# Keys of both head groups in one buffer, three key transfers a group, and the batch loop written out, in a two-layer attention kernel

## The reference

```python
# layer 0
xn = (x - mean) / jnp.sqrt(var + EPS) * gamma
qkv = jnp.einsum('oc,bcn->bon', w_qkv, xf)
sim = jnp.einsum('bhdi,bhdj->bhij', q, k) * scale
sim = sim + bias[None]
attn = _stable_softmax(sim)
out = jnp.einsum('bhij,bhdj->bhdi', attn, v)
out = jnp.einsum('oc,bcn->bon', w_out, out).reshape(B, C, H, W)
x1 = out + residual
# layer 1
attn = softmax(jnp.einsum('bno,bom->bnm', f, g), axis=2)
y = gamma1 * jnp.einsum('bci,bij->bcj', hh, attn) + x1
```

## Time and profile before

| | us |
|---|---|
| median of three runs | 1881.58 |
| lowest, highest | 1879.25, 1883.2 |
| span of the profiled execution | 1881.0 |

### The profile page before, as it was taken

The page is one execution under the profiler, slowest core; times in us unless marked ns, Lnnn a source line. Parts: engine busy times, 40 slices in busy tenths (PEclk is TensorE's granted clock), DMA queues, the critical chain, the costliest instruction groups (busy, mean ns, idle before and its releaser), DMA issues. The chain is left out here.

```text
span 1881.0 us, 23267 instructions
## 1 busy us (share of the span) xinstructions
PE 1642.2 (87%) x6545; PEld 805.5 (43%) x6545; DVE 1498.6 (80%) x2218; ACT 1388.9 (74%) x2043; POOL 0.2 (0%) x4
## 2 busy tenths in 40 slices
PE   6645989989988998989988999889989999889988
PEld 2133343535444453535444353535435354435424
DVE  4235988888878988789878989789878988789853
ACT  1135887878778887788778787778778787779853
POOL 0000000000000000000000000000000000000000
PEclk8667968999999999999999999999999999989999
DMA  1395103301042104301043102501043101500000
GB/s 57 58 221 156 33 25 105 110 19 39 24 138 77 57 1 127 111 1 57 24 108 107 57 1 85 149 5 57 1 128 110 43 15 53 142 20 26 16 30 23
DMA packets 72905, 123.04 MB, mean 65 GB/s; under 512 B 24042, under 2 KB 38954, under 8 KB 72746
## 3 DMA queue, kind: packets, MB, share of 16 engines
q1 hardware_dynamic: 72756, 121.29, 22.7%
HBM read 78.66 MB, written 44.13 MB: 65 GB/s over the span
## 5 line engine op out<-in xcount | busy, mean ns | idle before, releaser
L1117 DVE CUSTOM_DVE_ANT_0 biased<-psum,bias_lines_sb 128x1024 f32<-128x1024 f32 x512 | 618.0, 1222 | 209.1 <-issue 129.1
L915 ACT ACTIVATE biased<-biased,nmax 128x1024 f32<-128x1024 f32 x512 | 587.2, 1147 | 188.9 <-DVE nmax L1117 183.7
L1131 DVE TENSOR_TENSOR biased<-psum,bias_lines_sb 128x1024 f32<-128x1024 f32 x512 | 599.1, 1221 | 47.7 <-PE psum L715 37.1
L932 ACT ACTIVATE probs<-biased 128x1024 f32<-128x1024 f32 x512 | 536.0, 1056 | 132.7 <-DVE biased L1131 118.8
L688 PE MATMUL psum<-k_tail,q_stack 96*128 96x256 f32 x512 | 272.8, 533 | 120.3 <-DVE nmax L1117 50.6
L715 PE MATMUL psum<-q_stack,k_main 98*128 98x512 f32 x768 | 302.9, 502 | 38.9 <-DVE nmax L1117 15.1
L742 PE MATMUL psum<-probs,vT 128*32 128x512 f32 x2048 | 292.6, 642 | 4.9 <-DVE st L1008 2.7
L715 PEld LDWEIGHTS psum<-q_stack,k_main 98*128 98x128 f32 x768 | 137.2, 205 | 257.9 <-issue 112.6
L688 PEld LDWEIGHTS psum<-k_tail,q_stack 96*128 96x128 f32 x512 | 102.8, 201 | 305.7 <-DVE nmax L1117 172.5
L690 PE MATMUL psum<-k_main,q_stack 96*128 96x512 f32 x512 | 216.3, 422 | 0.0
L633 PE MATMUL psum<-probs 128*128 128x512 f32 x384 | 186.6, 592 | 0.0
(11 more groups left out here) (91 smaller groups left out, 1409.2 us busy)
## 6 DMA issues: line engine op xcount, KB each, us to landing
q_stack<-q_parts SPq DMA_DIRECT2D x96, 256.0 KB, 5.6
k_parts<-st SPq DMA_DIRECT2D x16, 1024.0 KB, 4.7
q_parts<-st SPq DMA_DIRECT2D x16, 1024.0 KB, 4.0
k_main<-k_parts SPq DMA_DIRECT2D x48, 256.0 KB, 5.3
xn<-in_x_dram SPq DMA_DIRECT2D x8, 1024.0 KB, 8.6
x<-in_x_dram SPq DMA_DIRECT2D x8, 1024.0 KB, 11.2
out_dram<-x SPq DMA_DIRECT2D x8, 1024.0 KB, 4.0
bias_lines_sb<-bias_lines SPq DMA_DIRECT2D x32, 240.0 KB, 20.6
```

Of the source, the lines that this page charges most:

```text
L915: nc.scalar.activation(biased[:, m % BIASED, :], biased[:, m % BIASED, :], ACT.Exp, scale=-1.0, bias=nmax[:, m:m + 1], accum_out=rowsum[:, ...
L932: nc.scalar.activation(probs[:, n % P_SLOTS], biased[:, n % BIASED, :] .rearrange("p (i n) -> p i n", i=2), ACT.Exp).then_inc(SEMS["probs_ ...
L1117: nc.vector.tensor_tensor_reduce(biased[:, m % BIASED, :], pair(bank_of(g, first, ("rows", m))), bias_lines[:, g * HG + h, a0:a0 + N], -1. ...
L1131: nc.vector.tensor_tensor(biased[:, n % BIASED, :].rearrange("p (i n) -> p i n", i=2), psum[:, bank:bank + 2, :], bias_lines[:, g * HG + 2 ...
```

## The change

`k_main` and `k_tail` become one buffer `k_stack`, with all 1024 keys of both groups. `k_in` is three transfers of 512 KB, issued in one go after `k_out`; its only wait on readers is for a columns phase of the batch before. A row tile has two products of 512 columns instead of three of 256, 256 and 512. In SP's program `k_out` and `k_in` of group 1 now stand ahead of the load of `xn`, and those of the next batch's group 0 stand whole in the rows phase of group 1. The loop over batches 1 to 6 is written out, with constant waits. The wait for `lines_loaded` is left out after the first batch.

```diff
-        KMAIN = 3 * N // 4
-        k_main = sb("k_main", [KS + 2, HG, KMAIN], F32R)
-        k_tail = sb("k_tail", [KS + 2, G, HG, N - KMAIN], F32R)
+        k_stack = sb("k_stack", [KS + 2, G, HG, N], F32R)
...
-        K_DMAS = 3 * 3 * 16
+        K_DMAS = 3 * 16
...
         def need(eng, name, b, n):
-            value = b * per_batch[name] + (start[name] + n)
-            if isinstance(value, int):
-                if value > 0:
-                    eng.wait_ge(SEMS[name], value)
-            elif eng is nc.sync:
-                need_beside(eng, (lines_stored, 16 * W), (name, b, n))
-            else:
+            value = b * per_batch[name] + n
+            if value > 0:
                 eng.wait_ge(SEMS[name], value)
...
-        def batches(eng, body):
-            body(0, first=True, last=False)
-            with eng.Fori(1, B - 1) as b:
-                body(b, first=False, last=False)
-            body(B - 1, first=False, last=True)
+        def batches(body):
+            for b in range(B):
+                body(b, first=(b == 0), last=(b == B - 1))
...
-            def k_in(b, g, chunk):
+            def k_in(b, g):
                 need(sp, "k_stored", b, 16 * (g + 1))
-                cols = slice(KCHUNKS[chunk], KCHUNKS[chunk + 1])
-                dst = k_main[:, :, cols] if cols.start < KMAIN else k_tail[:, g]
+                need(sp, "s_mm", b - 1, (g + 1) * SN)
                 for r, part in enumerate((0, 1, 0)):
-                    sp.dma_start(dst[r * HD:(r + 1) * HD].bitcast(F32),
-                                 k_dram.ap()[part, :, :, cols].rearrange("h d n -> d h n")).then_inc(k_loaded, 16)
+                    sp.dma_start(k_stack[r * HD:(r + 1) * HD, g].bitcast(F32),
+                                 k_dram.ap()[part].rearrange("h d n -> d h n")).then_inc(k_loaded, 16)
...
             def element(b, first, last):
                 q_out(b, 1)
                 q_in(b, 1, ("s_mm", b, 0))
+                k_out(b, 1)
+                k_in(b, 1)
                 if not last:
                     need(sp, "v_mm", b, NT)
                     need(sp, "qk_mm", b, split(1, 1))
                     sp.dma_start(xn[:], x_dram[b + 1]).then_inc(x_loaded, 16)
-                k_out(b, 1)
-                k_in(b, 1, 2)
                 for r in range(NHALF):
                     shift_to_stack(b, 0, r)
-                for chunk in range(2):
-                    columns_done(b, 0, chunk)
-                    k_in(b, 1, chunk)
                 if not last:
                     k_out(b + 1, 0)
-                    need(sp, "s_mm", b, SN)
-                    k_in(b + 1, 0, 2)
+                    k_in(b + 1, 0)
                 for r in range(NHALF):
                     shift_to_stack(b, 1, r)
...
                     q_out(b + 1, 0)
                     q_in(b + 1, 0, ("s_mm", b, SN))
-                if not last:
-                    for chunk in range(2):
-                        columns_done(b, 1, chunk)
-                        k_in(b + 1, 0, chunk)
                 residual_in(b)
...
-                pe.matmul(psum[:, bank, 0:keys], lhsT, tail[:, ::-1], start=True, stop=True)
-                pe.matmul(psum[:, bank, keys:HALF], lhsT, back(main, 0, HALF - keys, KMAIN), start=True, stop=True)
-                pe.matmul(psum[:, bank + 1, :], lhsT, back(main, HALF - keys, HALF, KMAIN), start=True,
+                keys = k_stack[0:KS, g, h, :]
+                pe.matmul(psum[:, bank, :], lhsT, back(keys, 0, HALF, N), start=True, stop=True)
+                pe.matmul(psum[:, bank + 1, :], lhsT, back(keys, HALF, HALF, N), start=True,
                           stop=True).then_inc(SEMS["a_mm"], 1)
...
-                        need_beside(dve, (lines_loaded[g * HG + h], 16 * ROWS), ("a_mm", b, g * A_TILES + m + 1), free)
+                        if first:
+                            dve.wait_ge(lines_loaded[g * HG + h], 16 * ROWS)
+                        need(dve, *free)
+                        need(dve, "a_mm", b, g * A_TILES + m + 1)
```

More of the change, by code:

```diff
@@ L201, in two_layer_attention @@
         SEMS = {name: s for name, (s, k) in credit.items()}
-        start = {name: k * (2 if name in ("s_mm", "bias_added", "probs_ready") else 1)
-                 for name, k in per_batch.items()}
         def need(eng, name, b, n):
-            value = b * per_batch[name] + (start[name] + n)
-            if isinstance(value, int):
-                if value > 0:
-                    eng.wait_ge(SEMS[name], value)
-            elif eng is nc.sync:
-                need_beside(eng, (lines_stored, 16 * W), (name, b, n))
-            else:
-                eng.wait_ge(SEMS[name], value)
[L219 to L225, removed]
+            value = b * per_batch[name] + n
+            if value > 0:
+                eng.wait_ge(SEMS[name], value)
         A_TILES = HG * NT
@@ L338, in column_tile @@
             return half, t, j
-        KCHUNKS = (0, N // 2, KMAIN, N)
         LEAD = 3
@@ L355, in _ @@
         def _(sp):
-            for name in ("x_loaded", "res_loaded", "q_stored", "q_loaded", "k_stored", "k_loaded", "rows_loaded",
-                         "y_stored"):
-                sp.sem_inc(SEMS[name], start[name])
             sp.dma_start(xn[:], x_dram[0]).then_inc(x_loaded, 16)
@@ L444, in _ @@
             q_out(0, 0)
-            for chunk in (2, 0, 1):
-                k_in(0, 0, chunk)
+            k_in(0, 0)
             q_in(0, 0, ("s_mm", -1, SN))
@@ L453, in _ @@
                                  .rearrange("x a w -> x (a w)")).then_inc(lines_loaded[h], 16)
-            def columns_done(b, g, chunk):
-                need(sp, "s_mm", b, g * SN + (SN - SN // NHALF) + KCHUNKS[chunk + 1] // P * HP)
             def element(b, first, last):
@@ L484, in element @@
                     q_in(b + 1, 0, ("s_mm", b, SN))
-                if not last:
-                    for chunk in range(2):
-                        columns_done(b, 1, chunk)
-                        k_in(b + 1, 0, chunk)
                 residual_in(b)
-            batches(sp, element)
+            batches(element)
             result_out(B - 1)
-            sp.wait_ge(y_stored, 16 * (B + 1))
+            sp.wait_ge(y_stored, 16 * B)
         @block.tensor
         def _(pe):
-            for name in TENSOR:
-                pe.sem_inc(SEMS[name], start[name])
             pe.wait_ge(weights_loaded, 16 * N_WEIGHTS)
@@ L685, in row_tiles @@
                 lhsT = q_stack[0:KS, g, t * P // HALF, h, t * P % HALF:t * P % HALF + P]
-                main, tail = k_main[0:KS, h, :], k_tail[0:KS, g, h, :]
-                keys = N - KMAIN
-                pe.matmul(psum[:, bank, 0:keys], lhsT, tail[:, ::-1], start=True, stop=True)
-                pe.matmul(psum[:, bank, keys:HALF], lhsT, back(main, 0, HALF - keys, KMAIN), start=True, stop=True)
-                pe.matmul(psum[:, bank + 1, :], lhsT, back(main, HALF - keys, HALF, KMAIN), start=True,
+                keys = k_stack[0:KS, g, h, :]
+                pe.matmul(psum[:, bank, :], lhsT, back(keys, 0, HALF, N), start=True, stop=True)
+                pe.matmul(psum[:, bank + 1, :], lhsT, back(keys, HALF, HALF, N), start=True,
                           stop=True).then_inc(SEMS["a_mm"], 1)
@@ L697, in rows_phase @@
                     beside(g, "rows", m, b, first, last)
[L699 to L702, removed]
             def columns_phase(b, g, first, last):
@@ L714, in columns_phase @@
                             for i in range(2):
-                                mm = pe.matmul(psum[:, bank + i, :], key_tile(g, 2 * j + i, t),
+                                mm = pe.matmul(psum[:, bank + i, :], k_stack[:, g, 2 * j + i, t * P:(t + 1) * P],
                                                q_stack[:, g, NHALF - 1 - half, 2 * j + i, ::-1],
@@ L786, in element @@
                     columns_phase(b, g, first, last)
-            batches(pe, element)
+            batches(element)
             for kind, arg, b in alone(LAYER_1):
@@ L794, in _ @@
             nc.scalar.preload_act_table_set("natural_log_exp_and_others")
-            for name in SCALAR:
-                act.sem_inc(SEMS[name], start[name])
             def do(kind, arg, b, g, first, last, tail=False):
@@ L940, in element @@
                     output(b, 1, 1, last)
-            batches(act, element)
+            batches(element)
             for kind, arg, b in alone(LAYER_1):
@@ L947, in _ @@
         def _(dve):
-            for name in VECTOR:
-                dve.sem_inc(SEMS[name], start[name])
             nc.vector.memset(mean_w[:], 1.0 / C)
-            nc.vector.memset(k_main[KS:KS + 2].bitcast(F32), 1.0)
-            nc.vector.memset(k_tail[KS:KS + 2].bitcast(F32), 1.0)
+            nc.vector.memset(k_stack[KS:KS + 2].bitcast(F32), 1.0)
             nc.vector.memset(eps_col[:], EPS).then_inc(consts_set, 1)
@@ L1136, in element @@
                             do(kind, arg, e, g, first, last)
-            batches(dve, element)
```

(3 more changed lines are left out.)

## The result

| | us |
|---|---|
| changed kernel, median of four runs (lowest, highest) | 1922.53 (1918.44, 1923.02) |
| kernel before, median in the same comparison | 1881.53 |
| ratio, with its 95% interval | 1.0216 (1.0201 to 1.0230) |
| span of the changed kernel's profiled execution | 1921.2 |

The account below looks back on a forecast made before the run. No engine was taken as the bound all through; group 1's rows phase was bound by PE's columns, and PE stopped for `k_main` at seven batch ends. 1881.0 - 52.5 + 99 = 1927.5, said as 1928 us, range 1899 to 1944.

Parts of the forecast that it names:

- late `xn`, waits: Rows phase of group 0: PE waits for `xn`, queued behind key store and loads, 12.0 us a batch, 84 in all.
- late `xn`, over the waits: After the wait for `xn`, PE works at the lower clock and loses 2.5 us in each of batches 1 to 6.
- ends of the batches: At seven batch ends PE's wait for `k_main` and the low clock after it go: 52.5 us gained.
- loop written out: Loop over batches 1 to 6 with constant waits: no gain taken, 2 us at most.
- two products a tile: Row tiles as two products instead of three: 512 tiles give nothing, since the third weight load is hidden.
- The chain of the landing: Group 0's rows phase: store 4.0 us, fixed part 2.2, keys 7.0, `xn` 2.9, so `xn` lands at 800.7.
- The rival of keys at full rate: Key loads before `xn` run at 355 GB/s: 1910 us, 1900 with half of the clock's loss as well; chance 0.18.
- Sum: 7.5 us for each of 7 ends: Batch ends: 4.7 us of PE's wait plus 2.8 us of products lost at half clock.
- No wait is left on PE: Batch end: queries there at 961.1 and PSUM bank free at 960.8, PE free at 961.5; 4.7 us go.
- The check by VectorE's four tiles: Batch end on DVE: first maximum 5.3 us earlier, first to fourth 2.3 us less; together 7.6 us.
- So the register arithmetic lies beside the work: Group 1's rows phase takes 60.20 us written out in batch 7, 60.30 in the loop's batch 3; nothing taken.
- The faster rival: `xn` is served beside the keys, a wait of 6 us without loss of clock: 1871 us; chance 0.06.

Follow-up runs that it names:

- experiment 4: Kernel before with its loop over batches written out and nothing else changed: 1869.57 us, 0.9938 of the kernel before.
- the first experiment: Changed kernel with the load of `xn` ahead of group 1's key store and key loads again: 1825.75 us, 0.9705 of the kernel before.
- experiment 3: Changed kernel with row tiles as three products again, of 256, 256 and 512 columns: 1922.16 us, 1.0222 of the kernel before.
- experiment 2: Changed kernel with the load of `xn` between group 1's key store and key loads: 1859.28 us, 0.9887 of the kernel before.
- experiment 6: Changed kernel with `xn` ahead of group 1's key store and loads, and the kernel before's loop and register waits kept: 1838.04 us, 0.9765 of the kernel before.

## Why the prediction was right, and where it was not

| term | forecast | measured |
|---|---|---|
| late `xn`, waits | 84 | 82.6 (88.8 less 6.2) |
| late `xn`, over the waits | 15 | 14.2 |
| ends of the batches | -52.5 | -43.8 (experiment 4 to 1) |
| loop written out | 0 | -12.0 |
| two products a tile | 0 | +0.4, within the noise (part of the ends' -43.8) |
| sum | +46.5 | +41.0 |

- *The late `xn`.* Right in place and size: 96.8 us by the first experiment, against 99. The chain of the landing (4.0 for the store, 2.2 fixed, the keys' bytes, 2.9 for `xn`) gave 16.1 us after the key store; PE starts at 16.4. The keys moved at 216 GB/s, a little under the 226 that I took from the bias lines. The rival of keys at full rate is wrong for these loads. The 358 GB/s that the prediction took from the Trainium skill (DMA: Bandwidth & Descriptors, section Specifications) is not reached by them.
- *The clock.* The windows show it at 0.50 after the long wait, and 14.2 us over the waits in six batches is 2.4 each, against 2.5. In the window of batch 4 PE works 4.8 us at half speed, and half of that is 2.4. That this excess is the clock's is the reading of the windows; no run held the clock up to test it.
- *The ends of the batches.* The mechanism held, the size did not: "Sum: 7.5 us for each of 7 ends". With both kernels written out, the difference between experiments 4 and 1 is 43.8 us, 6.3 for each end. Two terms were mis-sized. "No wait is left on PE" is not so: 33.8 us of waits went, but 4.3 for the PSUM bank came, 0.6 at each end, since the bank comes free with the third of the last four adds and not with the second, as I had read. And what lies over the waits is (43.8 - 33.8 + 4.3) / 7 = 2.0 us for each end, where I took 2.8 for the clock. The check by VectorE's four tiles (6.1 us against 3.8) seemed to confirm that term, but part of the difference was the loop: over the five ends behind a taken branch it is 6.2 on average, and 5.5 at the same ends written out. The 43.8 us also hold the two products, the wait for `lines_loaded` left out and the `dynamic_dma_scratch_size=1024` that the changed kernel sets; of these only the products were tested by themselves.
- *The loop.* "So the register arithmetic lies beside the work" holds for the rows phases, which take 60.2 us in the loop and out of it; "I take nothing" was the step that failed, by 12 us. I compared whole phases inside the loop with the same phases of batch 7, which can't show a cost at the seam between two iterations. There it was, hidden in part by the stall that I read at the same place and put down wholly to the DMA and the clock. The two errors have opposite signs, and most of them cancel: 52.5 against 55.8. That the total came out 5.5 us from the forecast is in this part luck.
- *The row tiles.* Nothing beyond the noise, as forecast, by experiment 3.
- *The faster rival* had `xn` served beside the keys. It was not: it was used 11.2 us after its issue, and alone it would take about 5. Its condition, a wait for `xn` of less than 7.5 us with the clock's part, is met in experiment 2, with 3.6 us on average in batches 1 to 6, and there the kernel is indeed 1.1% faster than before. So the sign hung on one line's place.

## What to carry to other kernels

In a queue that is issued in order, look at what a moved wait stands in front of, and when that is needed: here 1 MB of input with 0.2 us to spare was put behind a store, its landing and 1.5 MB of keys, and lost more than the removed stall gave. The same edit with two parts of SP's program swapped turns 2% slower into 3% faster. Where a loop ends, read the rows of its branch and of the instruction behind it on each engine, as well as those of the waits: a stall there can hide the cost of the loop, which then comes out as a gain of whatever removes either.

## What the runs showed of the hardware

- A loop whose branch was taken cost 2.4 to 3.0 us of the kernel's time for each taken branch (12 us for five, 9.1 for three fewer, 12.3 for five). TensorE's taken branch took 3.3 to 3.8 us in the kernel before and 0.2 in experiment 6, an untaken one 83 ns; the next instruction on VectorE's sequencer came 3.2 to 3.4 us behind its branch in experiment 6 and 7.0 to 7.3 in the kernel before.
- Loads of 32 partitions issued one on the other moved at 215 to 226 GB/s, with rows of 2, 4 and 7.5 KB alike, at a DMA share of 1.00 and more; a stretch of 3 us with `xn` and the key store, transfers of 128 partitions with rows of 4 KB, moved at 355 GB/s in the kernel before. Whether the number of partitions makes the difference no run here tests.
